# The last context tile brought in turned, and one small transfer asked for earlier, in a Perceiver block

## The reference

```python
x = x + xattn(layernorm(x), ctx_2048, mask)   # scores = x @ ctx.T / sqrt(D), masked, softmax, @ ctx
x = x + attn(layernorm(x), Wq, Wk, Wv, Wo)    # 16 heads, causal within the 32 tokens of a batch
x = x + ffn(layernorm(x), w_gate, w_up, w_down)  # silu(x @ gate.T) * (x @ up.T) @ down.T, hidden 4096
```

## Time and profile before

| | us |
|---|---|
| median of 3 runs | 1468.44 (1467.93 to 1469.58) |
| the profiled execution's own time | 1468.63 |
| its span | 1466.8 |
| PE busy | 1448.6 (99%) |
| DVE, ACT, POOL busy | 724.4, 542.5, 868.9 |
| HBM read | 112.78 MB, at 80 GB/s over the span |

### The profile page before, as it was taken

One profiled execution on the slowest core, in us unless ns is written; L12 is line 12 of the kernel. 1 busy time (PEld: TensorE's weight loads), 2 busy tenths in 40 slices (PEclk: granted clock), 3 DMA queues, 4 the chain that ended last, 5 costly groups with the idle time before them and its releaser, 6 DMA issues.

```text
span 1466.8 us, 24774 instructions
## 1 busy us (share of the span) xinstructions
PE 1448.6 (99%) x8862; PEld 1181.8 (81%) x8862; DVE 724.4 (49%) x1019; ACT 542.5 (37%) x1059; POOL 868.9 (59%) x704
## 2 busy tenths in 40 slices
PE   7999999999999999999999999999999999999998
PEld 5666898888988888888888888888888888888886
DVE  4777133141240769472562652644735626526437
ACT  3456242231321453333434343344334343333442
POOL 1333221212113131878978879879789788798795
PEclk9999999999999999999999999999999999999999
DMA  9994210201001000211112112112121121121113
GB/s 382 409 410 175 76 36 29 83 30 59 30 30 58 2 23 8 69 38 60 57 50 64 50 50 71 37 53 75 36 57 57 50 64 50 57 65 46 47 57 114
DMA packets 43404, 117.86 MB, mean 80 GB/s; under 512 B 4945, under 2 KB 5329, under 8 KB 40401
## 3 DMA queue, kind: packets, MB, share of 16 engines
q1 hardware_dynamic: 42912, 116.60, 22.9%
q10 hardware_dynamic: 432, 0.39, 0.1%
HBM read 112.78 MB, written 4.19 MB: 80 GB/s over the span
## 4 chain that ended last, share of the span: by engine, by line
PE 95%; DVE 2%; DMA 1%; issue 1%; SPq 1%; ACT 0%; DVEq 0%
PE ps L1551 39%; PE ps L1571 19%; PE ps L1071 10%; PE ps L1073 10%; PE ps L1072 10%; PE ps L1130 2%; PE ps L1178 2%; PE ps L1153 1%; PE ps L1077 1%; DMA ext_cols<-in_ext 1%; SPq L404 1%; PE ps L1262 1%; DVE x L2056 1%; PE ps L1345 1%; PE ps L1304 0%
## 5 line engine op out<-in xcount | busy, mean ns | idle before, releaser
L634 POOL TENSOR_TENSOR b_lo<-blk,b_hi 128x512 fp32r<-128x512 f32 x180 | 231.6, 1294 | 50.2 <-ACT b_hi L966 40.9
L547 POOL TENSOR_TENSOR w_lo<-raw,w_hi 128x2048 fp32r<-128x2048 f32 x16 | 73.6, 4600 | 258.1 <-ACT w_hi L765 258.1
L2056 DVE TENSOR_TENSOR x<-ps,x 128x1024 f32<-128x1024 f32 x195 | 224.3, 1207 | 0.0
L1551 PE MATMUL ps<-xT_hi,b_hi 128*128 128x512 f32 x480 | 186.7, 389 | 0.0
L1551 PE MATMUL ps<-xT_lo,b_hi 128*128 128x512 f32 x480 | 186.7, 389 | 0.0
L1551 PE MATMUL ps<-xT_hi,b_lo 128*128 128x512 f32 x480 | 186.7, 389 | 0.0
L1571 PE MATMUL ps<-b_hi,b_hi 128*128 128x512 f32 x420 | 166.7, 397 | 0.0
L1571 PE MATMUL ps<-b_lo,b_hi 128*128 128x512 f32 x420 | 163.8, 390 | 0.0
L1571 PE MATMUL ps<-b_hi,b_lo 128*128 128x512 f32 x420 | 163.7, 390 | 0.0
L634 POOL TENSOR_TENSOR b_lo<-s_sum,b_hi 128x512 fp32r<-128x512 f32 x105 | 136.0, 1295 | 35.9 <-ACT b_hi L966 35.9
L2019 DVE TENSOR_TENSOR hid<-ps,kept 128x512 f32<-128x512 f32 x60 | 41.5, 691 | 233.9 <-PE ps L1551 194.0
(11 more groups left out here) (180 smaller groups left out, 3142.9 us busy)
## 6 DMA issues: line engine op xcount, KB each, us to landing
blk<-in_blocks SPq DMA_DIRECT2D x180, 256.0 KB, 2.7
ctx<-in_ctx SPq DMA_DIRECT2D x64, 512.0 KB, 11.2
raw<-in_w SPq DMA_DIRECT2D x19, 1024.0 KB, 4.8
x<-in_x SPq DMA_DIRECT2D x8, 512.0 KB, 14.8
out<-x SPq DMA_DIRECT2D x16, 256.0 KB, 2.6
lT_most<-in_turned SPq DMA_DIRECT2D x3, 1032.0 KB, 11.0
lT_most<-in_turned SPq DMA_DIRECT2D x3, 774.0 KB, 9.4
cT<-in_turned SPq DMA_DIRECT2D x1, 1032.0 KB, 4.7
```

What stands on the lines that cost most here:

```text
L547: pool.tensor_tensor(w_lo[wslot][:, :], raw[slot][:, :], w_hi[wslot][:, :].bitcast(F32), ALU.subtract).then_inc(split_done[slot], 1)
L634: pool.tensor_tensor(b_lo[slot][:, :], src[:, :], b_hi[slot][:, :].bitcast(F32), ALU.subtract).then_inc(block_lo, 1)
L1551: mm = pe.matmul(ps[:, bank, :], stat[a], moving[b], start=first and m == 0, stop=(s == 3 and m == 2), skip_group_check=True)
L2056: dve.tensor_tensor(part, ps[:, bank:bank + 2, :], part, ALU.add).then_inc(down_added, 1)
```

## The change

`LOADED` loses chunk 0 of tile 2, which PE now turns, and gains chunks 1 and 2 of tile 7, so that PE turns nothing of tile 7. Of these, chunks 0 and 1 go into `lT[0]` and `lT[1]`, chunks 2 and 3 into `cT[1]` and `cT[2]`. SP asks for `ext_cols` ahead of tile 1. For tile 7 it asks for both `lT` chunks ahead of the plain first half, for `raw[0]` and the other two chunks behind it, and for the plain second half last; `readout(7)` waits for the plain halves itself. PE's last round is written out: `turn_rows(1)`, `scores_of(7, 0)` and `scores_of(7, 1)` stand ahead of `readout(6)`, and PSUM banks of `turn_rows` and of the last readout are others. `row_normalise(1)` on ACT moves into the round t = 5, and DVE's `spread_extra(7)` moves ahead of `add_readout(6)`.

```diff
-LOADED = ((2, 0), (3, 0), (4, 0), (5, 0), (6, 0), (7, 0), (7, 3))
+LOADED = ((3, 0), (4, 0), (5, 0), (6, 0), (7, 0), (7, 1), (7, 2), (7, 3))
...
-        ROW_BANKS = (6, 6, 0, 2, 6, 2, 6, 2)
-        LAST_READOUT = 0
+        ROW_BANKS = (6, 0, 2, 6, 0, 6, 0, 6)
+        LAST_READOUT = 2
+        LAST_SLOT = {2: 1, 3: 2}
...
             def loaded(t):
                 for n, (tile_of, j) in enumerate(LOADED):
-                    if tile_of == t and j == 0:
+                    if tile_of == t and j < 2:
                         if n > 1:
                             there = LOADED[n - 2]
                             sync.wait_ge(scores_done, there[0] * KP + there[1] + 1)
...
+            sync.dma_start(ext_cols[:, :, :], ext_in).then_inc(ext_full, 16)
             tile(1)
-            sync.dma_start(ext_cols[:, :, :], ext_in).then_inc(ext_full, 16)
             tile(2)
-            loaded(2)
-            for t in range(RING, NT):
+            for t in range(RING, NT - 1):
...
+            t = NT - 1
+            sync.dma_start(x[:, t, :], x_in[:, t, :]).then_inc(x_full[t % 4], 16)
+            loaded(t)
+            sync.wait_ge(half_read, t - RING + 1)
+            for b in range(BT):
+                context(t, 0, b).then_inc(ctx_full[t % RING][0], 16)
+            sync.dma_start(raw[0][:, :], w_in[0]).then_inc(raw_full[0], 16)
+            for j in (2, 3):
+                sync.wait_ge(scores_done, 1 + max(c for c in range(NT * KP) if by_pe(c) and c % RING == LAST_SLOT[j]))
+                sync.dma_start(cT[LAST_SLOT[j]][:, :, :, :], turned_in[LOADED.index((t, j))])\
+                    .then_inc(turned_full[LOADED.index((t, j))], 16)
+            sync.wait_ge(readout_done, t - RING + 1)
+            for b in range(BT):
+                context(t, 1, b).then_inc(ctx_full[t % RING][1], 16)
...
                 if t == 6:
-                    row_normalise(1)
                     row_normalise(2)
-                    act.wait_ge(scores_done, LOADED[-2][0] * KP + 1)
+                    act.wait_ge(scores_done, (NT - 1) * KP + 2)
                     pair_split(0, 0)
                 context(t + 1, 3)
                 if t == 5:
                     row_hi(0)
+                    row_normalise(1)
...
                 for h in range(2):
+                    if t == NT - 1:
+                        pe.wait_ge(ctx_full[t % RING][h], (t // RING + h) * BT * 16)
...
             def turn_rows(t):
                 pe.wait_ge(xn_ready, t + 1)
-                if t < 2:
-                    pe.wait_ge(readout_free, 6 + t)
-                elif t < 4:
+                if t == 0:
+                    pe.wait_ge(readout_free, 6)
+                elif t < 3:
                     pe.wait_ge(c_act_done, act_before(NT * KP))
                     pe.wait_ge(c_dve_done, dve_before(NT * KP))
+                    if t == 2:
+                        pe.wait_ge(next_act_done, NT)
+                        pe.wait_ge(next_dve_done, NT)
+                elif t == 3:
+                    pe.wait_ge(readout_free, NT - 1)
+                    pe.wait_ge(xt_ready, 1)
...
-            for t in range(NT - 1):
+            for t in range(NT - 2):
...
-                if t == 6:
-                    turn_rows(1)
                 scores_of(t + 1, 2)
-                if t == 6:
-                    turn_rows(2)
                 scores_of(t + 1, 3)
+            next_turn(NT - 1)
+            turn_rows(1)
+            scores_of(NT - 1, 0)
+            probabilities(NT - 2)
+            scores_of(NT - 1, 1)
+            readout(NT - 2)
+            scores_of(NT - 1, 2)
+            turn_rows(2)
+            scores_of(NT - 1, 3)
             turn_rows(3)
             turn_rows(4)
             probabilities(NT - 1)
...
+                    else:
+                        spread_extra(t + 1)
                     add_readout(t)
                     row_stats(t)
...
-                if t + 2 == NT:
-                    spread_extra(t + 1)
```

More of the change, by code:

```diff
@@ L1118, in context @@
                     if before is not None:
[L1119 to L1122, removed]
                         if b < by_act(before):
@@ L1141, in scores_of @@
                     n = LOADED.index((t, j))
-                    pe.wait_ge(turned_full[n], 16 + (n % 2 * 16 if j == 0 else 0))
+                    pe.wait_ge(turned_full[n], 16 + (n % 2 * 16 if j < 2 else 0))
                 if j == 0:
@@ L1147, in scores_of @@
                         pe.wait_ge(scores_read, t)
-                src = lT[n % 2] if not by_pe(c) and j == 0 else [cT[c % RING][:, b] for b in range(BT)]
+                slot = c % RING if by_pe(c) else LAST_SLOT.get(j)
+                src = lT[n % 2] if not by_pe(c) and j < 2 else [cT[slot][:, b] for b in range(BT)]
                 for e in range(2):
```

## The result

The changed kernel takes 1460.61 us (median of 6 runs, 1459.89 to 1461.53), the kernel before 1468.24 in the same comparison; the ratio is 0.9948 (95% interval 0.9935 to 0.9961), 7.6 us faster. 1460.8 had been forecast. The profiled execution took 1461.31 us with a span of 1459.5, against 1468.63 and 1466.8: 7.3 us less.

What follows compares the result with a forecast made beforehand. PE was taken as the bound, busy 99% of the span, with one 7.1 us wait behind ext_cols and DVE's chain at the end. The lead of 7.7 us at readout(7) gave 1468.6 - 7.7 = 1460.9, median 1460.8; range 1458.8 to 1463.8.

Steps and rivals of the forecast that it cites:

- The wait removed: Tile 1: with ext_cols early, PE's 7.1 us wait and the low clock go; context(1, 2) starts 8.5 us ahead.
- The chunk of tile 2: Tile 2: PE turns chunk 0 itself, 1.9 us more; readout(1) starts 6.5 us ahead; the stream loses 1032 KB, 2.6 us.
- The two streams: Tiles 3 to 6: PE 6.5 us and data 2.6 us earlier, room of 1.4 us at tile 6, cost nothing.
- The end: Tile 7, end of cross attention: DVE sets the pace; readout(6) 7.0 us ahead, readout(7) 7.7 us ahead.
- step 5: Transfers of tile 7: PE waits for chunks (7, 2) and (7, 3), scores end at 123.2, costing nothing.
- after 124: Sign of a wrong prediction: the scores of tile 7 ending later than 124 us.
- low clock again: Rival: PE, working some 5 of 9.5 us before readout(7), drops its clock, about 1.7 us; total 1463, chance 0.10.
- The lead into the second stage: From readout(7) into the second stage: all is 7.7 us ahead, then PE is full with unchanged work.
- the rule weighed: DVE operations with SBUF inputs and GpSimd ones reading SBUF exclude each other; fills(7) priced clear at 0.6 us, softmax 2.0.

Runs made afterwards that it cites:

- experiment 9: The kernel before with 60 unread identity transposes in PE's first wait, for the exp of tile 0, ext_cols as late as before: 1466.81 us, ratio 0.9986.
- experiment 1: The kernel before with only the request for ext_cols moved ahead of tile 1: 1463.38 us, ratio 0.9966.
- experiment 3: The changed kernel with chunk 0 of tile 2 loaded again instead of turned by PE: 1463.47 us, ratio 0.9963.
- experiment 2: The changed kernel with only the request for ext_cols put back behind tile 1: 1469.17 us, ratio 1.0006.
- experiment 7: Experiment 6 with DVE doing fills(7) before spread_extra(7), in its wait for POOL: 1459.40 us, ratio 0.9941.
- experiment 8: Experiment 7 with row_hi(1) on ACT and row_lo(1) on DVE also formed in that wait for POOL: 1458.41 us, ratio 0.9928.
- experiment 4: The changed kernel with 22 unread identity transposes on PE behind readout(6), in its wait for chunk (7, 2): 1460.07 us, ratio 0.9942.
- experiment 6: The changed kernel with SP's tile 7 order altered: (7, 0), plain first half, (7, 1), (7, 2), (7, 3), raw[0], plain second half: 1460.73 us, ratio 0.9947.
- experiment 5: The changed kernel itself, unaltered, timed again beside experiments 6, 7 and 8: 1461.60 us, ratio 0.9950.

## Why the prediction was right, and where a step was wrong

1. *The wait removed.* Right. 7.1 us of wait and some 1.6 of low clock went (experiment 9 measures the second by itself), and no wait of like length took their place. The term was 0.7 small: PE came to the probabilities at 24.3, not at 25.1, since the last batch of tile 1's first half was no later than before.
2. *The chunk of tile 2.* Right. PE is 9.2 us ahead in front of it and 7.5 behind it; it cost 1.7 us where 1.9 and 0.1 for the banks had been reckoned. ACT and DVE kept up.
3. *The two streams.* Right, and it is the part without which the change would have been worth 2 to 3 us less (experiments 1 and 3). The four transfers of tile 6's second half were over at 96.4 (80.88 and 15.5 us), PE wanted them at 97.2: 0.8 us of room, where 1.4 had been reckoned with PE 1 us later. Experiments 1 and 3 leave the 1032 KB in the stream, and there PE comes to `context(6, 2)` at 99.1 and 100.2, the second with 1.1 us of low clock in it. The stream, full at 409 GB/s, then sets the pace of the cross attention.
4. *The end.* Right, where the clock stayed up. The forecast has 17.5 us from `next_turn(7)` to `readout(7)` (110.1 to 127.6) where it was 18.8 before; experiments 2 and 3 have 17.8 and 17.6. So two chunks less for PE bring some 1 us of their 3.9, because DVE's chain is what ends last. That it does shows in experiments 7 and 8, where DVE is relieved: 16.5 and 15.6 us. `fills(7)`, priced clear of POOL's split, took 0.4 us more than reckoned, and the softmax 0.2 less than its 2.0. The changed kernel took 19.15 us; the rest of the difference is step 5.
5. *The transfers of tile 7.* This step failed. It said that PE's waits for (7, 2) and (7, 3) cost nothing, as the scores would be over at 123.2, 0.8 us before DVE; it named "after 124" as a sign of being wrong, and 124.7 was measured. The hole in the stream was foreseen, and so was the order of the landings; but the rest took 16.5 us from the request to (7, 2), not 15.1, PE wanted the chunk 0.7 us earlier than reckoned, and the wait was 2.7 us (1.6 forecast). Behind it the clock fell, the scores ended at 124.7, and DVE waited 1.25 us for them. The term that the step put at nothing is the clock: with as late a chunk and the clock up, experiments 2, 3 and 4 take 17.6 to 18.0 us, the two profiles of the changed kernel 19.15 and 18.9, and a chunk in time (experiment 6) gives no less than 18.0, of which POOL's split made 0.5. The rival "low clock again" was thus part of what happened, at 1 to 1.5 us and not 1.7, because DVE would have held PE in any case.
6. *The lead into the second stage.* Right. 139.75 to 132.60, 7.15 us, of the 7.3 by which the profiled executions differ.

The total came within 0.2 us by luck: 1 us more than forecast in steps 1 and 2 met a loss of 1 to 1.5 us in step 5, which left `readout(7)` 7.15 us ahead where 7.7 were forecast, and the medians lie 7.6 us apart where the profiled executions lie 7.3 (experiment 5 has the same kernel at 1461.60, 0.8 us above the forecast). The figure is better than its working.

On the rule weighed, from the Trainium skill ("SBUF — State Buffer", section "Who interferes with whom"): its direction holds here. `fill` took 0.69 us and the adding of the fill 0.86 in the changed kernel, where both ran into POOL's split, and 0.28 and 0.43 in experiment 7, where neither did. My schedule had `fills(7)` clear of it and was wrong: the first half of the split ran until 122.26 there, 0.5 us into it. `fill` was over at 122.41, 0.15 us behind that half, as it would be if it had been shut out until then.

## What to carry to other kernels

When one long wait is removed in a stage whose transfers run full, ask at once how far the data can follow; here the whole gain lasted only because 1032 KB were taken out of the early stream in the same edit (without that, 4.8 us in experiment 1 instead of 7.6). Work taken from an engine that doesn't end last is worth little until the chain that does is shortened: moving three small operations into DVE's idle 5 us (and one of ACT's ahead) brought 2.3 us by the medians of experiments 6 and 8, the 32 transposes some 1 us. And a wait that costs nothing by the sum may cost by the clock: keep waits of the requesting queue off the transfers that don't need them, or give the engine something to do.

## What was not expected of the hardware

A rest of PE of about 2.5 us may or may not bring the lower level of the clock. It fell behind waits of 2.70 and 2.47 us (changed kernel, twice) and 2.43 us (experiment 3), and stayed at 1.00 behind 2.45 us (experiment 1), 2.55 us (experiment 2) and 2.31 us (experiment 3, tile 7). What decides between the two was not tried and stays open. Each fall made the work behind the wait last 1.4 to 1.7 us longer. With useless transposes in the wait the clock stayed up in both places where they were tried. For the wait of 7 us that is clear; behind the one for (7, 2) the clock might in that one profile have stayed up without them.
